# Per-head transformer layer on eight cores: prologue interleaved with the first head, PSUM banks redistributed, normalisation work in one piece per row block, and a third stage behind a fence

## The reference, cut to what matters

```
h   = layernorm(x)
qkv = h @ w_qkv                                  # [2048, 6144]
q,k = layernorm_128(rope(q)), layernorm_128(rope(k))     # per head, scale and bias
a   = tril((q @ k.T) ** 4);  a = a / a.sum(-1)
x1  = x + layernorm(concat_heads(a @ v) @ w_out)
bw  = sign(weight) * mean(abs(weight), axis=1)   # per output row
out = x1 + layernorm(layernorm(x1) @ bw.T + bias)
```

## Time and profile before

| | |
|---|---|
| median of 3 runs | 2461.52 us (2454.68 to 2462.14) |
| the profiled execution | 2468.96 us, span 2467.2 us (slowest core) |
| spans of the 8 cores | 2420.4 to 2467.2 us, granted clock 0.818 to 0.828 |
| TensorE busy | 1648.3 us, 67% |
| ScalarE busy | 1195.0 us, 48% |
| VectorE busy | 1007.1 us, 41% |
| chain that ended last | TensorE 30%, DMA 23%, ScalarE 18%, issue 15%, VectorE 9% |

### The profile page before, as it was taken

One profiled execution on the slowest core, in us unless ns is written; L12 is line 12 of the kernel. 1 busy time (PEld: TensorE's weight loads), 2 busy tenths in 40 slices (PEclk: granted clock), 3 DMA queues, 4 the chain that ended last, 5 costly groups with the idle time before them and its releaser, 6 DMA issues.

```text
span 2467.2 us, 32956 instructions; the slowest of 8 cores (2420.4 to 2467.2 us)
## 1 busy us (share of the span) xinstructions
PE 1648.3 (67%) x8960; PEld 847.0 (34%) x8960; DVE 1007.1 (41%) x3706; ACT 1195.0 (48%) x2865; POOL 175.6 (7%) x217
## 2 busy tenths in 40 slices
PE   0007678887887887887888788547856550947870
PEld 0004344444544544454454444223322220413330
DVE  4663455554554555554455455420123130302214
ACT  0001376677567667657756766761425130522342
POOL 1010000000000000000000000000010111010001
PEclk9998878878967987887797797658977775979995
DMA  5685524633651562363266153295284759455324
GB/s 116 166 156 41 52 37 51 86 51 36 86 81 18 75 86 46 42 86 55 32 86 86 18 69 61 43 162 126 58 139 99 124 101 262 96 126 164 78 83 177
DMA packets 428500, 219.24 MB, mean 89 GB/s; under 512 B 403984, under 2 KB 403984, under 8 KB 424224
## 3 DMA queue, kind: packets, MB, share of 16 engines
q0 software_dynamic: 157856, 145.81, 32.4%
q1 hardware_dynamic: 270464, 71.33, 17.3%
HBM read 151.04 MB, written 49.28 MB: 81 GB/s over the span
## 4 chain that ended last, share of the span: by engine, by line
PE 30%; DMA 23%; ACT 18%; issue 15%; DVE 9%; SPq 2%; ACTq 1%; DVEq 0%; POOL 0%; POOLq 0%
PE PQ L345 21%; ACT S2B L467 8%; DMA APJ<-APJT 7%; DMA LNXT<-LNC 6%; DMA L2F<-LN2C 3%; DMA lnx2t_sc<-L2F 3%; PE PV L492 3%; PE PS L460 3%; ACT S4B L470 3%; PE PB L683 2%; PE PB L821 2%; ACT P4S L375 2%; DVE T L351 1%; DMA ATK<-lnx2t_sc 1%; DVE QR L366 1%
## 5 line engine op out<-in xcount | busy, mean ns | idle before, releaser
L345 PE MATMUL PQ<-WH,LNXT 128*128 128x384 bf16 x4096 | 740.1, 339 | 216.1 <-DMA WH<-wqkv 189.0
L345 PEld LDWEIGHTS PQ<-WH,LNXT 128*128 128x128 bf16 x4096 | 410.2, 101 | 509.1 <-issue 267.3
L492 PE MATMUL PV<-VPAD,S4B 128*128 128x129 bf16 x2176 | 279.2, 266 | 178.9 <-DVE S4B L474 102.8
L470 ACT ACTIVATE S4B<-S2B 128x512 bf16<-128x512 bf16 (+3 forms) x640 | 361.9, 566 | 59.6 <-ACT S2B L467 1.1
L821 PE MATMUL PB<-ATK,LNXT 128*128 128x512 bf16 x1024 | 239.4, 395 | 151.6 <-DMA ATK<-lnx2t_sc 80.3
L467 ACT ACTIVATE S2B<-PS 128x512 bf16<-128x512 f32 (+3 forms) x640 | 329.0, 514 | 0.8 <-PE PS L460 0.8
L375 ACT ACTIVATE P4S<-QR 128x128 f32<-128x128 f32 x512 | 153.5, 300 | 335.1 <-DVE QR L366 334.6
L460 PE MATMUL PS<-QFM,KFM 128*128 128x512 bf16 (+3 forms) x640 | 257.3, 433 | 85.8 <-ACT S2B L467 61.8
L683 PE MATMUL PB<-ATK,LNXT 128*128 128x512 bf16 x896 | 222.8, 404 | 123.9 <-ACT APJT L689 89.5
L492 PEld LDWEIGHTS PV<-VPAD,S4B 128*128 128x128 bf16 x2176 | 173.0, 113 | 335.9 <-issue 319.0
L474 DVE TENSOR_TENSOR S4B<-S4B,TRI 128x128 bf16<-128x128 bf16 x256 | 57.5, 225 | 429.8 <-ACT S4B L470 429.2
(11 more groups left out here) (88 smaller groups left out, 1100.4 us busy)
## 6 DMA issues: line engine op xcount, KB each, us to landing
WH<-wqkv POOLq DMA_DIRECT2D x48, 512.0 KB, 16.5
XB<-xb POOLq DMA_DIRECT2D x16, 1024.0 KB, 7.5
out<-O POOLq DMA_DIRECT2D x16, 1024.0 KB, 8.5
XB<-fw POOLq DMA_DIRECT2D x16, 512.0 KB, 20.1
swt_sc<-XB POOLq DMA_DIRECT2D x16, 512.0 KB, 17.7
LNXT<-wout POOLq DMA_DIRECT2D x1, 8192.0 KB, 57.4
XB<-xb POOLq DMA_DIRECT2D x16, 512.0 KB, 8.8
out_sc<-O POOLq DMA_DIRECT2D x16, 512.0 KB, 6.3
```

What stands on the lines that cost most here:

```text
L345: P.op("t", lambda t, m=m, kc=kc, par=par, b=b: t.matmul(PQ[b][:, 0:384], LNXT[:, kc * N + m * 128: kc * N + m * 128 + 128], WH[par][:, kc ...
L470: P.op("s", lambda s, jb=jb, j2=j2, nj=nj: s.activation(S4B[jb][:, 0:nj], S2B[j2][:, 0:nj], ACTF.Square), reads=[f"s2{j2}"], writes=[f"s4{ ...
L492: stop=stop: t.matmul(PV[bank][:, off:off + 129], S4B[jb][:, 128 * sub - s0: 128 * sub - s0 + 128], VPAD[par][:, j * 129: j * 129 + 129], ...
```

## The change

- Prologue: emitted block by block, with unit c of head 0's QKV projection directly behind block c. Sum of squares and the normalisation itself move from VectorE to ScalarE, with two more small VectorE steps (nm = -mean * rstd). `LNC` has two buffers. The loads of `WH` for heads 0 and 1 are issued ahead of the loads of x.
- PSUM: `PS` has two banks and not four, `PV` four and not two, one part to a bank. `S2B` 4 buffers (3 before), `S4B` 6 (5), `P4S` 4 (2), `OUTH` 2 (1).
- All 16 heads go through DRAM (`attnt_sc`), and stage B loads 16 planes and not 14.
- Stage B: the four sub-steps of a group become one `b_cl_unit`, emitted behind every fourth unit. The sum is a VectorE reduce in place of a ScalarE pass. `O1` two buffers (4), `LN2C` and `L2F` two (1). x and x1 are held in float32 (`XB2`, `out1_sc`). The group work of the last block follows behind the last unit of B.
- The weights of C come in one DMA behind that, then a fence, then stage C with its own tensors and `c_cl_unit` behind every fourth unit.

```diff
-    out1_h = nc.dram_tensor("out1_sc", [N, E], BF16, kind="Internal")
+    out1_h = nc.dram_tensor("out1_sc", [N, E], F32, kind="Internal")
...
-            PS = [TA(nc.psum_tensor(f"PS{i}", [128, 512], F32)) for i in range(4)]
-            PV = [TA(nc.psum_tensor(f"PV{i}", [128, 512], F32)) for i in range(2)]
+            PS = [TA(nc.psum_tensor(f"PS{i}", [128, 512], F32)) for i in range(2)]
+            PV = [TA(nc.psum_tensor(f"PV{i}", [128, 512], F32)) for i in range(4)]
...
-                    if hh < H - 2:
-                        akeys = [f"afm{par}/{b_}" for b_ in range(16)]
...
+                    akeys = [f"afm{par}/{b_}" for b_ in range(16)]
...
             emit_w(0)
             emit_w(1)
-            for h in range(H + 1):
+
+            uq0 = qkv_units(0)
+            for c in range(MC):
+                b = c % 2
+                xk = f"xb{b}"
+                P.dma("g", lambda g, c=c, b=b: g.dma_start(
+                    out=XB[b][:], in_=xh[c * 128:(c + 1) * 128, :]),
+                    writes=[xk], slot=xk)
+                P.op("v", lambda v, b=b: v.tensor_reduce(
+                    XS[:, 0:1], XB[b][:], AX.X, AOT.add),
+                    reads=[xk], writes=["xsum"])
+                P.op("s", lambda s, b=b: s.activation(
+                    SCR[:], XB[b][:], ACTF.Square, accum_out=XS[:, 1:2]),
+                    reads=[xk], writes=["xss", "scrA"])
+                ln_smalls(XS, "x", "xsum", "xss")
...
+                P.op("s", lambda s, b=b: s.activation(
+                    LNC[b][:], XB[b][:], ACTF.Identity, bias=XS[:, 7:8],
+                    scale=XS[:, 6:7]),
+                    reads=[xk, "xr", "xnm"], writes=[f"lnc{b}"])
+                P.dma("y", lambda y, c=c, b=b: y.dma_start_transpose(
...
+                uq0[c]()
+            for th in uq0[MC:]:
+                th()
+            emit_w(2)
+            swt_load(0)
+
+            for h in range(1, H + 1):
...
-            def b_cl_subs(tb, cl):
+            def b_cl_unit(tb, cl):
...
+                P.op("v", lambda v, cl=cl, tbb=tbb, b0=b0: v.tensor_reduce(
+                    BS[:, b0:b0 + 1], APJ[tbb][:, cl * E:(cl + 1) * E], AX.X,
+                    AOT.add), reads=apk, writes=[kp + "sum"])
+                P.op("s", lambda s, cl=cl, tbb=tbb, b0=b0: s.activation(
+                    SCB[:], APJ[tbb][:, cl * E:(cl + 1) * E], ACTF.Square,
+                    accum_out=BS[:, b0 + 1:b0 + 2]),
+                    reads=apk, writes=[kp + "ss", "scb"])
+                ln_smalls(BS, kp, kp + "sum", kp + "ss", b0=b0)
...
                 for s_ in range(16):
                     b_s_unit(tb, s_)
-                    if subs is not None:
-                        cl, si = s_ % 4, s_ // 4
-                        subs[cl][si]()
-                        if si == 3:
-                            load_xb2(tb * 4 + cl)
...
+                    if tb >= 1 and s_ % 4 == 3:
+                        cl = s_ // 4
+                        b_cl_unit(tb - 1, cl)
+                        load_xb2(tb * 4 + cl)
+            for cl in range(4):
+                b_cl_unit(3, cl)
+
+            P.dma("g", lambda g: g.dma_start(
+                out=AP(LNXT, 0, [[KC * N, 128], [N, 16], [1, N]]),
+                in_=AP(swt_h, 0, [[N, 128], [N * 128, 16], [1, N]])),
+                reads=[f"swtsp/{kc}" for kc in range(KC)],
+                writes=["woutP", "swtP"], slot="swtP")
+
+        P.fence()
...
+                P.op("v", lambda v, cl=cl, tbb=tbb, b0=b0: v.tensor_reduce(
+                    CS[:, b0:b0 + 1], YTM[tbb][:, cl * E:(cl + 1) * E], AX.X,
+                    AOT.add), reads=ymk, writes=[kp + "sum"])
...
+                    if tb >= 1 and s_ % 4 == 3:
+                        cl = s_ // 4
+                        c_cl_unit(tb - 1, cl)
+                        load_o1r(tb * 4 + cl)
+            for cl in range(4):
+                c_cl_unit(3, cl)
```

More of the change, by code:

```diff
@@ L210, in build_nc @@
         ALPHACC = TE(nc.sbuf_tensor("ALPHACC", [128, 16], F32))
[L211 to L216, removed]
+        C_ZERO, C_I128, C_I2048, C_EPS, C_TWO, C_ONE, C_NI2048 = \
+            0, 1, 2, 3, 4, 5, 6
         def cp(col):
@@ L266, in build_nc @@
             XB = [TA(nc.sbuf_tensor(f"XB{i}", [128, E], F32)) for i in range(2)]
-            LNC = [TA(nc.sbuf_tensor("LNC0", [128, E], BF16))] * 2
+            LNC = [TA(nc.sbuf_tensor(f"LNC{i}", [128, E], BF16)) for i in range(2)]
             XS = TA(nc.sbuf_tensor("XS", [128, 8], F32))
@@ new lines, in b_cl_unit @@
+                P.dma("g", lambda g, c=c, cb=cb: g.dma_start(
+                    out=out1_h[c * 128:(c + 1) * 128, :], in_=O1[cb][:]),
+                    reads=[f"o1{cb}"], writes=[f"o1sp/{c}"], slot=f"o1sp{cb}")
+                P.op("s", lambda s, cb=cb, b0=b0: s.activation(
+                    SCB[:], O1[cb][:], ACTF.Square,
+                    accum_out=BS[:, b0 + 1:b0 + 2]),
+                    reads=[f"o1{cb}"], writes=[kp + "ss", "scb"])
+                ln_smalls(BS, kp + "L2", kp + "sum", kp + "ss", b0=b0)
@@ new lines, in b_cl_unit @@
+                P.op("v", lambda v, cb=cb, b0=b0: v.tensor_scalar(
+                    LN2C[cb][:], O1[cb][:], BS[:, b0 + 2:b0 + 3],
+                    BS[:, b0 + 6:b0 + 7], AOT.subtract, AOT.mult),
+                    reads=[f"o1{cb}", kp + "L2m", kp + "L2r"],
+                    writes=[f"ln2c{cb}"])
+                P.dma("y", lambda y, cb=cb: y.dma_start_transpose(
+                    AP(L2F[cb], 0, [[KC * 128, 128], [128, 16], [1, 128]]),
+                    AP(LN2C[cb], 0, [[E, 128], [128, 16], [1, 128]])),
+                    reads=[f"ln2c{cb}"],
+                    writes=[f"l2f{cb}/{kc}" for kc in range(KC)],
+                    slot=f"l2fT{cb}")
@@ L765, in load_xb2 @@
+                P.dma("g", lambda g, c=c, cb=cb: g.dma_start(
+                    out=AP(lnx2t_h, c * 128,
+                           [[N, 128], [N * 128, 16], [1, 128]]),
+                    in_=L2F[cb][:]),
+                    reads=[f"l2f{cb}/{kc}" for kc in range(KC)],
+                    writes=[f"l2sp/{c}"], slot=f"l2sp{cb}")
             def load_xb2(c):
@@ L807, in load_lx @@
                            [[N, 128], [N * 128, 16], [1, 512]])),
[L808 to L815 removed]
+                    reads=["l2_done"], writes=[f"lx{tbb}"], slot=f"lx{tbb}")
             def c_s_unit(tb, s_):
@@ L837, in c_s_unit, with c_cl_unit @@
                       reads=[f"ytt{pb}"],
-                      writes=[f"ytm{tbb}/{cl}/{s_}" for cl in range(4)]
-                      + [f"apj{tbb}/{cl}/{s_}" for cl in range(4)],
+                      writes=[f"ytm{tbb}/{cl}/{s_}" for cl in range(4)],
                       slot=f"ytmTd{pb}")
-            def c_cl_subs(tb, cl):
+            def c_cl_unit(tb, cl):
                 tbb = tb % 2
```

322 lines of the change are left out of this document (116 added, 206 removed).

## The result

The changed kernel takes 2642 us (median of 9 runs) against 2461 us for the kernel before (10 runs): 1.072 times as long, 95% interval 1.069 to 1.075. In some executions the cores of one die show a lower granted clock and the time is some per cent longer; the ratios leave these out, and experiment 4 has one execution without it. It was forecast slower and it is, but by 181 us and not by 88, and outside my range.

What follows compares the result with a forecast made beforehand. No engine bounds the whole; each stage has its own limit. Prologue +154, attention +5, A to B +4, stage B +18, stage C and tail -93 sum to +88, giving 2549 us, range 2515 to 2585.

Steps and rivals of the forecast that it cites:

- Prologue, +154 forecast: Prologue: transposing, multiplying and evacuating strung together once per block; head 0's projection ends at 408 and not 254 us.
- a link: Prologue: one block's chain from one ScalarE square pass to the next, 21.3 us, 16 times, 341 us.
- the queue of weights: Prologue: six weight loads ahead of x in the same queue, 38 us, so x lands at 58 us.
- Attention with A to B, +9 forecast: Attention +5 us from two score banks; passage to stage B +4 us from the last plane and a longer ATK load.
- the pair that waits for a square: Attention: with two PS banks one score pair per head waits for ScalarE's square, 0.5 us, 15 times 7 us.
- Stage B, +18 forecast: Stage B: bound by the chain of group work and transposes, 22.5 us a group; 431 against 413 us.
- the failed step: Stage B: the last unit transpose lands 2.6 us after issue, and the next group waits for exactly that one.
- Stage C and tail, -93 forecast: Stage C 233 and not 311 us, group work covered by four PC banks; tail 48 and not 62.
- The shorter prologue: Rival, prologue: shorter link and x not waiting for weights, 70 us less, 2479 us; chance 0.12.
- the starved attention stage: Rival, attention: two score banks starve the stage, +43 us over the forecast's +5, 2592 us; chance 0.18.
- Stage B is bound by TensorE: Rival, stage B: unit transposes land before their group's chain ends, period 14 us, 2447 us, faster; chance 0.06.
- The opening section of the prediction: Kernel before, stage B: ScalarE's 88.3 us wait for a unit transpose put down to SyncE's in-order queue.

Runs made afterwards that it cites:

- experiment 4: Changed kernel with the prologue of the kernel before put back (one LNC buffer, head loop from 0): 2493 us, a single execution.
- experiment 9: Changed kernel with the QKV unit of block c-2 emitted after the normalising of block c, LNXT transposes counted in four semaphores: 2472 us, ratio 1.000.
- experiment 10: Changed kernel with the first two blocks of x loaded ahead of the six weight loads: 2613 us, ratio 1.061.
- experiment 6: Kernel before with the change's attention banks alone (two PS, four PV, each epilogue step waiting for its own part): 2465 us, ratio 0.999.
- experiment 1: Changed kernel with unit transposes of even and odd blocks counted in different semaphores, in stages B and C: 2470 us, ratio 1.005.
- experiment 3: Changed kernel without 12 of 16 loads of x in B and 12 of 16 reloads of the first output in C: 2552 us, ratio 1.038.
- experiment 5: Kernel before with only the semaphores of unit transposes in B and C split for even and odd blocks: 2326 us, ratio 0.941.
- experiment 2: Changed kernel with the residual x in B, the spilled first output and its reload in C held in bfloat16: 2618 us, ratio 1.065.
- the seam: Changed kernel with old prologue and even/odd semaphores, plus C following B without a fence, last groups between C's first units: 2313 us, ratio 0.934.

## Why the prediction was wrong

*Prologue, +154 forecast, +143 measured: right, with its mechanism.* x came at 52 and not 58 us (six loads cost 32 us and not 38), and from the first normalising pass at 57.1 us to the sixteenth at 381.4 a link took 21.6 us on the mean, with one slow transpose of 18.6 among them, against 21.3 and that one apart. The chain goes over VectorE's reduce and not over ScalarE's square, as I had summed it; the two end 0.2 us apart. That the product in the link is its cause is shown by experiment 9, which cut it and brought the end of the projection from 397 us to 189 to 201 on seven cores and 262 on the eighth; that the queue of weights stood in front of x, by experiment 10. A unit of 16 matmuls took 4.1 to 5.3 us after at least 12.6 us of idleness; the unit of 5.28 us at 204.83 had a granted clock of 0.50 throughout, the one of 4.21 at 183.98 a mean of 0.65. In experiment 9 (core 1) three units that begin 1.6 to 1.9 us after the end of the one before take 2.76; at 120.5 and 182.3 us the granted clock is 1.00 during such a unit. The rule of the Trainium skill that I had cited ("TensorE: Matmul & The Clock Gate", section on what is actually happening in the clock gate), that an array left idle falls back to 1.2 GHz and must be kept busy to come up again, agrees with both.

*Attention with A to B, +9 forecast, -22 measured: wrong in sign, small.* I charged 0.5 us a head for the pair that waits for a square. Experiment 6 shows that a wait of TensorE for a score bank is free there, and in its trace the banks shorten a head by 0.7 us; in the changed kernel a head is 87.4 us, 0.5 shorter. That is 7 to 10 us in all, by the traces only: the medians of experiment 6 lie 5 us apart, which can't be told from nothing. Another 10 us come from the first head (85 us in the changed kernel, 95 before). In the kernel before head 0's transpose of K landed after 15.6 us beside loads of weights, in experiment 4, with the same prologue, after 5.8; experiment 6, with the old loads, still has 97. So it looks like a matter of what runs beside it, and which part of the change moved that stays open. The last 5 us lie between head 15's transpose and B's first matmul, not looked into.

*Stage B, +18 forecast, +111 measured: the failed step.* Its words were "of which the last lands 2.6 us after its issue; and the next group waits for exactly that one, since a wait on a slot takes the newest". The second half was right and is shown by experiment 1. The first was mis-sized: the landing took 8.0 to 14.9 us, as the chain shows, which makes the group 30.6 us and not 22.5, eleven times, 88 us. The 2.61 of the earlier trace rows is ScalarE's idle time before a pass, from a stretch of stage C where only one transpose was under way (its landing took 2.41, at a DMA share of 0.27); on it I put 1.1 us for transfers twice as large. The same stage of the kernel before has loaded landings of the same transpose, in its chain of waits:

```profile
2214.14 2.41 DMA APJ<-APJT
...
2255.15 15.89 DMA APJ<-APJT
...
2335.41 13.81 DMA APJ<-APJT
```

The last two stand beside outputs of 1 MB and loads of 0.5 MB at a DMA share of 1.01. The forecast took the one that stood alone. Experiment 3 shows what should have been there: most of it is the load of x that GpSimd issues at that very moment. The Trainium skill ("DMA: Bandwidth & Descriptors", section on issuing engines that are not separate queues of the DMA) says that transfers of SyncE and of GpSimd run on the same 16 engines. The trace agrees with it (14.93 us to land at a DMA share of 0.91 from 1990.2 us on, 2.41 at 0.27), and I had not drawn on it. The earlier trace rows held a warning, with 5.5 us for a spill of half a megabyte by itself.

*Stage C and tail, -93 forecast, -60 measured: the same term.* The wait of 2.6 us per group was a landing of 6.8 to 15.1. With the wait gone (experiment 1) C and tail take 272 us, where I had 281.

*The rivals.* The shorter prologue and the starved attention stage did not come. "Stage B is bound by TensorE" was the case that mattered, for a reason I did not see: I held that SyncE's order put the transposes behind the group transpose. What held the groups was that they waited at all for transposes whose data they don't read. In experiment 1 B's units take 273 us, TensorE is busy for 239 of them, and the order in which SyncE is given its transposes is the same. The opening section of the prediction has the same fault: it put the 88.3 us of the earlier trace rows down to SyncE's queue, and experiment 5 took 62 of them away without touching that order. I had written down the rule of the newest slot and priced it, but not asked what the kernel would be without it, neither here nor in the kernel before, where it cost 144 us.

*The range.* I gave stage B bounds of 20.5 and 26 us a group, from the same landing. With the loaded landing of 15.9 us the upper end would have been 21.4 - 2.6 + 15.9 = 34.7 us a group, 134 us more than my 22.5, and the range would have held the result. The direction was right by the prologue and for the forecast's own reason. But 93 of the 181 us come from a landing that the forecast did not have.

## What to carry to other kernels

When several transfers share a semaphore, a wait that is computed when it is written down asks for all that were issued up to then, also those that belong to the next piece of work; give each generation its own semaphore before anything is reordered (here 6% of the whole, for two lines). Read how long a transfer takes to land from the place where it will stand, with what is issued beside it, and for the last of a batch, not for the median. A change that lays work closer together has to be measured again after each such repair, and its parts one by one: here the seam, put back after the repair, was worth 20 us, and the new stages, which differ from the old in several ways at once, gained 38 us in C and cost 53 in B.

## What was not expected of the hardware

- A unit transpose of 128 x 512 lands 2.4 to 2.6 us after issue with nothing beside it (stage C before, DMA share 0.27), 4.3 to 5.2 beside the spill of a group (experiment 3), and 8.0 to 14.9 with a load of 1 MB as well (the changed kernel).
- A load that converts float32 to bfloat16 landed no sooner than one that doesn't (medians in stage B: 9.6 us in experiment 2 and 9.8 in the changed kernel, for 1 MB read), though it writes half as much.
- In experiment 9 one core of eight had transfers in the prologue that took twice as long as on the others (transposes 19.3 against 7.8 to 8.3 us, medians), and its stage ended 61 us or more after theirs.
